# Local transformer on one core: look-back columns cleared between GpSimd's two rotations, and ScalarE's inverse norms behind the first two copies of the next step where a gate came before

## The reference

```python
def attn_layer(x, Wqkv, qs, ksc, Wo):
    q, k, v = split(x @ Wqkv)                  # 16 heads of 64
    q = l2norm(q) * qs
    k = l2norm(k) * ksc
    q = q * cos * scale + rotate_half(q) * sin * scale
    k = k * cos * inv + rotate_half(k) * sin * inv
    out = local_attention(q, k, v)             # windows of 32, each sees itself and the one before
    return out @ Wo
for i in range(6):
    x = attn_layer(shift_tokens(x), Wqkv[i], ...) + x
    x = ffn_layer(shift_tokens(x), ...) + x    # layernorm, W1, gated by gelu, W2
```

## Time and profile before

| | us |
|---|---|
| median of three runs | 2628.64 (2627.93 to 2630.3) |
| the profiled execution, its own time | 2627.98 |
| its span, first to last instruction | 2626.1 |
| PE busy | 2444.7 (93%) |
| DVE busy | 2174.8 (83%) |
| ACT busy | 2025.0 (77%) |
| GpSimd busy | 1536.7 (59%) |
| mean granted clock of PE | 0.98 |

### The profile page before, as it was taken

One profiled execution on the slowest core, in us unless ns is written; L12 is line 12 of the kernel. 1 busy time (PEld: TensorE's weight loads), 2 busy tenths in 40 slices (PEclk: granted clock), 3 DMA queues, 4 the chain that ended last, 5 costly groups with the idle time before them and its releaser, 6 DMA issues. The chain is left out here.

```text
span 2626.1 us, 118521 instructions
## 1 busy us (share of the span) xinstructions
PE 2444.7 (93%) x52349; PEld 1964.5 (75%) x52349; DVE 2174.8 (83%) x2455; ACT 2025.0 (77%) x4031; POOL 1536.7 (59%) x1075
## 2 busy tenths in 40 slices
PE   6799999999999999999999999689999999997999
PEld 2478888888787888788888887467777767775787
DVE  5788888888788888888898887388888988885888
ACT  4688888888888888888888887566667666764676
POOL 3788888888788888888897885122323222322111
PEclk8899999999999999999999999899999999999999
DMA  3243434443343344334333333122222222221221
GB/s 99 53 94 92 106 77 94 96 108 83 83 96 97 81 98 100 97 84 95 96 96 78 85 82 76 36 54 52 60 59 61 56 56 59 57 53 34 82 73 41
DMA packets 275793, 202.00 MB, mean 77 GB/s; under 512 B 117569, under 2 KB 215881, under 8 KB 274249
## 3 DMA queue, kind: packets, MB, share of 16 engines
q1 hardware_dynamic: 275280, 194.42, 30.8%
HBM read 36.96 MB, written 1.11 MB: 14 GB/s over the span
## 5 line engine op out<-in xcount | busy, mean ns | idle before, releaser
L509 POOL TENSOR_TENSOR lt_t_sin<-lt_qk,lt_tab 128x512 f32<-128x512 f32 x384 | 684.2, 1802 | 229.2 <-DVE lt_qk L1278 226.7
L514 POOL TENSOR_TENSOR lt_qr<-lt_qr,lt_t_sin 128x1024 f32<-128x1024 f32 x192 | 456.5, 2377 | 28.7 <-POOL lt_t_sin L509 1.8
L2047 DVE TENSOR_REDUCE fa_neg_max<-bank 128x1 f32<-128x1024 f32 x256 | 301.6, 1220 | 94.4 <-PE bank L1855 93.6
L1879 PE MATMUL bank<-fa_prob_t,fa_v 32*64 32x128 f32 x16384 | 279.6, 275 | 29.7 <-issue 25.1
L1969 ACT ACTIVATE fa_prob<-bank,fa_neg_max 128x1024 f32<-128x1024 f32 x128 | 142.7, 1114 | 210.5 <-DVE fa_neg_max L2047 164.3
L2057 DVE STREAM_TRANSPOSE fa_prob_t<-fa_prob 128x1024 f32<-128x1024 f32 x256 | 302.1, 1219 | 0.0
L1879 PEld LDWEIGHTS bank<-fa_prob_t,fa_v 32*64 32x64 f32 x16384 | 241.9, 131 | 77.1 <-issue 55.7
L602 PE MATMUL bank<-lt_w_high,lt_x_high 128*128 128x512 f32 x576 | 280.0, 486 | 0.8 <-ACT lt_v_tok L997 0.4
L1278 DVE TENSOR_TENSOR lt_qk<-lt_qk,lt_rn 128x2048 f32<-128x2048 f32 x96 | 254.5, 2651 | 24.3 <-ACT lt_rn L991 23.0
L619 PE MATMUL bank<-ident,lt_qr 128*128 128x128 f32 x1536 | 233.8, 276 | 13.6 <-POOL lt_qr L514 7.5
L970 ACT COPY lt_qk<-bank 128x512 f32<-128x512 f32 x384 | 229.7, 599 | 16.5 <-POOL lt_t_sin L509 3.8
(11 more groups left out here) (259 smaller groups left out, 5926.0 us busy)
## 6 DMA issues: line engine op xcount, KB each, us to landing
lt_v<-lt_v_tok SPq DMA_DIRECT2D x576, 128.0 KB, 2.4
fa_v<-fa_v_tok SPq DMA_DIRECT2D x256, 128.0 KB
lt_v<-lt_v_tok SPq DMA_DIRECT2D x192, 64.0 KB, 2.1
lt_k_t<-lt_k_t SPq DMA_DIRECT2D x84, 128.0 KB, 2.6
lt_v<-lt_v SPq DMA_DIRECT2D x168, 64.0 KB, 2.1
lt_w_raw<-in_lt_wqkv_dram SPq DMA_DIRECT2D x36, 256.0 KB, 3.3
ex_cw_all<-cw_kept SPq DMA_DIRECT2D x8, 1024.0 KB, 4.5
lt_x_s<-h_in SPq DMA_DIRECT2D x96, 64.0 KB, 2.7
```

The costliest lines, as they stand in the source:

```text
L509: pool.tensor_tensor(dst[:, :, i, :], src[:, :, 1 - i, :], tab[:, g // 2 % 2, 1, at:at + 32].unsqueeze(1).to_broadcast([P, HEADS, 32]), AL ...
L514: pool.tensor_tensor(qr[:, g % 2, half], qr[:, g % 2, half], t_sin[:, :], ALU.add).then_inc(S.rotated, 1)
L1879: mm = pe.matmul(bank[d, 4 + a, 0:P].rearrange("p (u r) -> p u r", u=UPQ), v[rows, half % 2, kb, d], prob_t[rows, q % 2, par, :, 32 * kb:3 ...
L2047: dve.tensor_reduce(neg_max[:, u % 2, par:par + 1], bank[:, 2 * par:2 * par + 2, :].rearrange("p a n -> p (a n)"), AX.X, ALU.max, negate=T ...
```

## The change

Two calls are moved, and nothing else is changed.

- In GpSimd's list, `clear_look(i + 1)` stands ahead of `rotate(i + 1, 1)` and no longer behind it and `scale_tables(c)`.
- In ACT's list, `invert_norms(i + 2)` stays at the end of a step where the step has no gate. Where it has one (`even(i, 5)` is not None), the call is left out there and made in the next step, which is even, behind the first two copies (T0 and Q0), as `invert_norms(i + 1)` with the same block number.

```diff
                         if k % WCH < 4:
                             split_low(k)
+                    if live(i + 1) and i + 1 >= SLOTS and not has_look(i + 1):
+                        clear_look(i + 1)
                     if live(i + 1):
                         rotate(i + 1, 1)
                     if c is not None and c >= 2:
                         scale_tables(c)
-                    if live(i + 1) and i + 1 >= SLOTS and not has_look(i + 1):
-                        clear_look(i + 1)
...
                             empty_turned(i, j)
                         if live(i + 2):
                             empty_qk(i + 2, j)
+                        if j == 0 and live(i + 1) and even(i - 1, 5) is not None:
+                            invert_norms(i + 1)
...
                         last_shift(4)
-                    if live(i + 2):
+                    if live(i + 2) and even(i, 5) is None:
                         invert_norms(i + 2)
```

## The result

The changed kernel takes 2703.69 us (median of four, 2699.77 to 2708.28) against 2629.47 for the kernel before, 74 us more by the medians. The ratio on record is 1.0275, interval 1.0255 to 1.0295: slower. The profiled execution took 2703.13 with a span of 2701.3, 75.2 more than before's.

A forecast was written before the change was run, and what follows sets the result against it. PE sets the pace, with GpSimd's chain as critical where it splits a weight between rotations. 50 (overtaking) + 2.5 (split) + 7 (plain) - 1 (copy) + 11 (clock) = 70 on 2628.6: about 2698 us, own range 2678 to 2716.

The forecast's parts named there:

- The norms 1.70 later: Even steps such as 42: DVE's normalising multiply L1278 starts 1.70 us later, 2.87 behind T0; 1.04 later in step 84.
- PE loses 0.17 in an even step: Projections of even steps: Q3 waits for Q1's later copy, PE loses 0.17 us; 0 in the later kind, as 84.
- DVE's slack hides its own delay: DVE's waits before L1298 (0.26) and L1349 (1.51), 1.77 us together, keep its later work in time.
- The overtaking: 14 split steps: DVE's multiply goes ahead of GpSimd's second sum, T2 3.6 us late instead of 1.7; 50 us.
- rival (1): GpSimd keeps its turn, or DVE comes too late or early for it: +28 us, 2657; chance 0.27.
- Plain steps: Even steps without a split: 0.3 us lost at +1.04, 0.5 at +1.70; 7 us with the clearing.
- The even steps with a stall of their own: Six plain even steps lengthened by PE stalls lose nothing; six long split steps lose 2.5 us together.
- Rival (3): Nothing measurable: waits on PE shorten "issue" stalls that came anyway, most of 60 us in this stretch; 2630, chance 0.06.
- The clock: PE at half clock behind the 3.6 us waits: 0.8 us in each of 14 steps, 11 us, bounds 0 and 24.
- The clearing: Ten memsets ahead of the second rotation: 1 us in plain even steps; the late ACT copy goes, PE gains about 1.

The follow-up runs named there:

- the control: The kernel before, with DVE's normalising multiply made to wait until both rotation sums of the block before are done: 0.9992 (0.9978 to 1.0007).

## Why the prediction was right

Forecast 2698, measured 2703.7, the forecast's own mechanism. By its steps:

- **The norms 1.70 later.** Said: L1278 2.87 behind T0. Measured: 807.03 - 804.16 = 2.87. Right.
- **PE loses 0.17 in an even step.** T0 of 43 came 14.80 behind T0 of 42 and not 14.70: 0.10. A little too much.
- **DVE's slack hides its own delay.** Said: 1.77 of waits hide it, so DVE's later work is in time. Half right. The wait before L1351 fell from 64.6 to 24.5 us over the stretch, and PE is not idle for DVE (one wait of 0.5 us at L677). But only 0.26 of the 1.77 stood before the row maxima: the first of them starts 8.83 us into an even step and not 7.79 (medians). PE's list waits for the subtraction behind it, and the stalls hang together with that (below).
- **The overtaking.** Said: T2 3.6 late in 14 steps, less what they lose today, the sum 4.3 long. Measured: 13 sums 4.20 long, T2 5.7 behind T0 each time, which is 3.43 late in step 43 and 2.66 to 3.45 in all. The margin was 0.30 us, from DVE's 819.97 to the end of the sine multiply at 820.27, where 0.2 was said. The fourteenth, 74, was lengthened by a stall to 15.7 us, as six others had been before. The run with one wait more on DVE showed the cause: the same lateness without the overtaking costs half. That run is also rival (1), forecast at +28 us: it is +37 when made to happen.
- **Plain steps.** Said: 0.3 and 0.5. Measured: 0.46 to 0.51 in ten steps of both kinds and once 0.78; behind the others next to nothing.
- **The even steps with a stall of their own.** Said: those "lose nothing", and six long split steps lose 2.5 together. This step failed. T2 behind them is indeed no more than 0.2 late, but the stall itself grows. The even steps together are 13.4 us longer, and 13.3 of that lies in the 21 that last over 15 us now: of the other 24, half gain the 0.10 and half lose as much. Rival (3) held the stalls of the odd steps against the waits, with 60 us of them; that is close to the row of the weight loads (PEld L677, 58.4), while PE itself was idle for "issue" for 29.7 us at L677 and L648 there. The 7 us for plain steps are 14 when they are moved alone.
- **The clock.** 11 us, with 0 to 24 as bounds. The trace has 54.6 us at half clock in the stretch and the kernel before 20.5; half of the difference is 17 us. Ten of the 13 long waits were followed by it.
- **The clearing.** No wait for the memset is left, and the time is that of the norms alone. Right, within what can be told.

By the trace the 72.9 us of the stretch are 45 of waits for the sum (46.8 less 1.8), 15 of half clock in odd steps (44.4 us there less 13.7, halved) and 13 of longer even steps, which hold the rest of the clock. That is 74 together, 1 more than measured; the half for the clock is the roughest of them. The prediction had 58 for waits, which was too much, 11 for the clock, too little, and nothing for the stalls. The total came out 6 us short because these go against each other; the terms were sized less well than the total shows.

**What stays open** is the proof of why late norms lengthen the stall; the order of events is in the traces. In PE's list the values' matmuls (L677) stand behind a wait for DVE's first subtraction (`S.shifted`, line 672 of the kernel). Here it is in step 12, before and after, and then the record of that wait in the changed kernel (engine, count, ns, start):

```profile
291.04 0.69 DVE L1300 TENSOR_TENSOR lt_prob<-bank,lt_row_max 128x512 f32<-128x512 f32 x1
```

```profile
304.35 0.69 DVE L1302 TENSOR_TENSOR lt_prob<-bank,lt_row_max 128x512 f32<-128x512 f32 x1
```

```profile
L672 PEldq EVENT_SEMAPHORE  x1: 51/51/51, 305.1 to 305.1; - x1
```

The wait is over 10.34 us into the step and not 9.06. PE itself doesn't stand still, since it still has matmuls in hand. But the next packet of instructions starts 1.1 us behind this wait in both kernels, at 11.43 and at 10.19, and PE's stall ends 1.4 us behind the landing of that packet in both (12.41 to 13.78, 11.40 to 12.78). In step 12 of all fourteen traces the packet starts 1.1 to 1.6 us behind the wait. Of PE's stalls over 0.4 us at L648, L659 and L677 in the stretch, all 26 in the kernel before and 35 of 36 in the changed one end 1.1 to 1.8 us behind the landing of the latest such packet. Over the even steps the wait is over at 9.30 in the median before, 10.34 after and 9.77 with the norms behind one copy, where the even steps were only 2 us longer. So the stall fits this: the wait holds back PE's list, the list holds back its next instructions, and where they are needed early PE runs dry. No run moved this wait, or the packets, alone, so it is argued and not shown. The total of idle named "issue" at L677 and L648 doesn't separate the kernels: 32.0 to 45.7 us without moved norms, 36.0 to 49.9 with them.

## What to carry to other kernels

Moving work behind other work on an engine with time to spare costs what the next engine in the chain can't spare: follow the result from engine to engine until someone has slack, step kind by step kind, since here the slack was 0.08 us in one kind and 0.7 in another. Where two engines hold each other up, as GpSimd and DVE did here, a few tenths of lateness can swap the order of two long instructions, and the price jumps by the length of one of them. If one of the two must go first, say so with a semaphore: the side that would have been held up anyway loses nothing by waiting (0.9992 in the control). And an engine that never stands idle for another can still be late for it: look at the waits in its list too, and not only at its idle time.

## What the runs showed of the hardware

- DVE's multiplies L1280 and L1287 and GpSimd's multiplies and sums did not run at once in these timelines, and the one that already waited went ahead of the other engine's next instruction, even if that is issued only 0.14 us behind the last. The wait is inside the record of the instruction: 2.38 becomes 4.20, 1.27 becomes 3.33. The order was the same in all 13 cases. This was in the trace before for another pair.
- A wait of PE of 3.26 us was followed by 3.4 us at half clock (0.51 of 2.4 GHz) or 6.8 us in ten of 13 cases. In the kernel with DVE's wait, where the same pause is 1.42 us, no half clock came behind it, and the whole stretch had 20.5 us, no more than the kernel before. The six pieces of half clock in the kernel before came behind pauses of 1.7 to 2.2 us, so shorter pauses than 3.26 were followed by it too. Keeping a pause short can be worth more than its own length.
- Idle of PE with no engine named, inside runs of small matmuls, ended 1.1 to 1.8 us behind the landing of a 16 KB packet of its instructions in 61 of 62 cases (stalls over 0.4 us, kernel before and changed kernel).
